# Sums of weight blocks formed from tiles already loaded, whole-tile weight loads, joins moved to the low-rank bank, four added transfers moved, one sum in four on GpSimd

## The reference, cut to what matters

```
# x: 8 batches x 512 x 2048, fp32.  R = 16
x = x + (x @ B0[i].T) @ A0[i].T                    # adapter i, one per batch
x = x + x @ W + (x @ lora_A[k]) @ lora_B[k]        # W: 2048 x 2048, adapter k per batch
```

## Time and profile before

| | |
|---|---|
| median of 3 runs | 1443.02 us (1441.91 to 1444.8) |
| profiled execution, its own time | 1451.56 us |
| its span, first to last instruction | 1449.9 us |
| TensorE busy | 1329.0 us, 92% of the span, 5684 matmuls |
| VectorE, ScalarE, GpSimd busy | 954.1, 459.2, 205.2 us |
| mean granted TensorE clock | 0.961 of full speed |
| DMA traffic | 350.93 MB, mean 242 GB/s |

### The profile page before, as it was taken

How to read it: one execution, slowest core, us unless ns; L and a number is a source line. 1 busy time by engine, 2 the same in 40 slices (tenths; PEclk the granted TensorE clock), 3 DMA queues, 4 the chain that set the end, 5 groups by cost and what they waited for, 6 DMA issues and landing times.

```text
span 1449.9 us, 15615 instructions
## 1 busy us (share of the span) xinstructions
PE 1329.0 (92%) x5684; PEld 1084.3 (75%) x5684; DVE 954.1 (66%) x1041; ACT 459.2 (32%) x536; POOL 205.2 (14%) x360
## 2 busy tenths in 40 slices
PE   6999999989788899996979999999989779999796
PEld 4888888877566688875768888888868558888585
DVE  4355755357666676765565766887877477788685
ACT  3232223222122332230322343334334235433342
POOL 3101000120123110102211100010112210100022
PEclk9999999999989999998989999999999989999899
DMA  8865843399999877888896373597898998945367
GB/s 306 283 224 168 284 145 95 110 275 361 332 373 337 276 272 255 268 280 317 275 321 218 117 246 116 181 357 249 324 348 227 249 282 213 229 150 175 94 178 170
DMA packets 140575, 350.93 MB, mean 242 GB/s; under 512 B 17476, under 2 KB 67652, under 8 KB 139476
## 3 DMA queue, kind: packets, MB, share of 16 engines
q1 hardware_dynamic: 103876, 237.01, 49.2%
q0 software_dynamic: 36624, 112.94, 26.0%
HBM read 236.55 MB, written 114.36 MB: 242 GB/s over the span
## 4 chain that ended last, share of the span: by engine, by line
PE 61%; DMA 20%; DVE 10%; issue 3%; SPq 2%; ACT 2%; POOL 1%; DVEq 0%; POOLq 0%; ACTq 0%
PE ps L2397 29%; PE ps L1247 25%; DMA w_raw<-in_W 4%; DMA wq<-in_W 3%; DMA w_ops<-job 2%; DMA w_sum<-w_raw 2%; PE ps L1220 2%; PE ps L2355 2%; DMA stage_all<-c_kept 2%; DMA job<-in_W 2%; DMA w_raw<-w_sum 1%; DVE w_lo L892 1%; ACT w_hi L733 1%; DMA lr_raw_q<-lrw 1%; PE ps L1178 1%
## 5 line engine op out<-in xcount | busy, mean ns | idle before, releaser
L1247 PE MATMUL ps<-b_hi,w_hi 128*128 128x512 f32 x896 | 359.1, 401 | 55.7 <-DVE w_lo L892 51.8
L1247 PE MATMUL ps<-b_lo,w_hi 128*128 128x512 f32 x896 | 355.6, 397 | 0.0
L1247 PE MATMUL ps<-b_hi,w_lo 128*128 128x512 f32 x896 | 354.9, 396 | 0.0
L2397 PE MATMUL ps<-b_hi,w_hi 128*128 128x512 f32 x784 | 311.3, 397 | 20.7 <-DVE val L2263 6.8
L2397 PE MATMUL ps<-b_lo,w_hi 128*128 128x512 f32 x784 | 310.0, 395 | 0.0
L2397 PE MATMUL ps<-b_hi,w_lo 128*128 128x512 f32 x784 | 309.7, 395 | 0.0
L1247 PEld LDWEIGHTS ps<-b_hi,w_hi 128*128 128x128 f32 x896 | 172.7, 193 | 100.6 <-DVE w_lo L892 58.8
L733 ACT CAST w_hi<-w_raw 128x1024 fp32r<-128x1024 f32 x88 | 92.5, 1051 | 422.1 <-PE ps L1247 203.2
L892 DVE TENSOR_TENSOR w_lo<-w_raw,w_hi 128x1024 fp32r<-128x1024 f32 x88 | 107.7, 1224 | 166.4 <-ACT w_hi L733 166.3
L1247 PEld LDWEIGHTS ps<-b_hi,w_lo 128*128 128x128 f32 x896 | 172.4, 192 | 37.1
L1247 PEld LDWEIGHTS ps<-b_lo,w_hi 128*128 128x128 f32 x896 | 172.6, 193 | 35.9
(11 more groups left out here) (151 smaller groups left out, 1186.0 us busy)
## 6 DMA issues: line engine op xcount, KB each, us to landing
w_raw<-in_W SPq DMA_DIRECT2D x88, 512.0 KB, 7.6
w_raw<-w_sum SPq DMA_DIRECT2D x56, 512.0 KB, 5.6
wq<-w_ops SPq DMA_DIRECT2D x56, 512.0 KB, 5.6
xq<-in_xT SPq DMA_DIRECT2D x44, 512.0 KB, 5.7
w_ops<-job POOLq DMA_DIRECT2D x40, 512.0 KB, 5.9
out_y<-stage POOLq DMA_DIRECT2D x40, 512.0 KB, 6.5
x_raw<-in_xT SPq DMA_DIRECT2D x32, 512.0 KB, 7.1
job<-in_W SPq DMA_DIRECT2D x24, 512.0 KB, 8.3
```

The lines of the kernel that those rows point to most:

```text
L1247: last = pe.matmul(bank[:, :], w[n % 2][:, c, t * P:(t + 1) * P], x[:, 2 * j + c, :], start=(j == 0 and c == 0 and w is w_hi and x is b_hi ...
L2397: last = pe.matmul(out, w[:, h, c, col:col + P], b[x], start=(po in (Q1, Q2, Q5, Q3) and c == 0 and i == 0), stop=(c == 3 and i == 2), ski ...
```

## The change

The jobs no longer load anything. The weight tiles of the second pair's units (56 to 111) are exactly the quarter blocks, so each stays in a place until its sums are made in it: 4 `w_raw` buffers, 3 tiles `w_more`, and for stretches of time 4 tiles in `u3`, in `x_raw[X12]` and in `x_raw[X11]`. A loop run when the program is built gives each unit a place, planning that it is free 3 units before its own. `load_weights(n + 3)` stands at the end of SyncE's iteration n and waits until the sum that was in the place is stored and read. VectorE makes js3, js1 and js2 (42 instructions) in iterations 4 to 7 of each product, GpSimd makes js4 (14 instructions) in front of its store. The additions of the identity in the jobs go, since the tiles have it already. In `two_level` a weight is one DMA of 1 MB with one semaphore, in runs of 8 KB, and the halves of a split are taken as columns of it (`w_half`). Joins write bank 1 (`p_ps`), the bank of the separate low-rank tiles, and the fourth comes one unit earlier. Four of the eight added transfers move from M6 to M3.

```diff
+    JOB_TILE = {js3: 0, js1: 4, js2: 6, js4: 2}
+    JOB_WHEN = {(js3, 0): 4, (js3, 1): 5, (js1, 0): 5, (js2, 0): 6, (js1, 1): 6, (js2, 1): 7, (js4, 0): 8, (js4, 1): 8}
+    LAST_READ = {js3: js2, js1: js1, js2: js4, js4: js4}
...
+    job_sums = {}
+    for o in range(PRODUCTS):
+        for (k, e), late in JOB_WHEN.items():
+            job_sums.setdefault(min(unit(1, o, late), LAST - 1), []).append((o, k, e))
...
+    PLACES = RAWS + 3 + 4
+    IN_U3, IN_X12, IN_X11 = "u3", "x12", "x11"
+    place_of, region_of, place_uses = {}, {}, [[] for _ in range(PLACES)]
+    free = [unit(1, P1, 0) - 2] * RAWS + [unit(0, P4, 7)] * 3 + [0] * 4
+    for n in range(unit(1, P1, 0), LAST):
+        o, u = at(n)[1:]
+        k, e = next((k, u - first) for k, first in JOB_TILE.items() if u - first in (0, 1))
+        gone = max(min(unit(1, o, JOB_WHEN[k, e]), LAST - 1) + 2.5, min(unit(1, o, JOB_WHEN[LAST_READ[k], e]), LAST - 1) + 1)
+        best = None
+        for i in range(PLACES):
+            t = i - RAWS - 3
+            regions = [(0, LAST + 9, None)] if t < 0 else [
+                (unit(1, P1, 0) + (-2 if t < 2 else 2), unit(1, P7, 3 if t < 2 else 7), IN_U3),
+                (unit(1, P7, 1 if t < 2 else 2), unit(1, P5, 1), IN_X12), (unit(1, P5, 0) - 2 + t, LAST + 9, IN_X11)]
+            for begins, ends, region in regions:
+                key = region is None, free[i], i, region
+                if free[i] <= n - 3 >= begins and gone <= ends and (best is None or key[:3] < best[:3]):
+                    best = key
+        _, _, i, region = best
+        place_of[n], region_of[n] = i, region
+        place_uses[i].append(n)
+        free[i] = gone
...
+    def w_came(n):
+        if n in place_of:
+            i = place_of[n]
+            before = len(raw_plan[i::RAWS]) if i < RAWS else 0
+            return w_loaded[i], 16 * (before + place_uses[i].index(n) + 1)
+        return w_loaded[main_raw(n)], 16 * (raw_of[n] // RAWS + 1)
...
+    def place_free(n):
+        _, o, u = at(n)
+        k, e = next((k, u - first) for k, first in JOB_TILE.items() if u - first in (0, 1))
+        return [sum_stored(n), (job_subtracted if LAST_READ[k] == js4 else job_summed, job_no[o, LAST_READ[k], e])]
+    def region_free(i, region=None):
+        return place_free([n for n in place_uses[i] if region_of[n] == region][-1])
...
-        def store_job(i, k):
-            o, h, _, _ = jobs[i]
-            tile, s, t = job_use(i, JOB_SUM[k])
-            pool.wait_ge(job_summed, job_no[i, k])
-            pool.dma_start(w_ops[o, k, :, h, :, :], tile).then_inc(job_stored[s][t], 16)
+        def store_job(o, k, e):
+            n = unit(1, o, JOB_TILE[k] + e)
+            if k == js4:
+                pool.wait_ge(job_summed, job_no[o, js2, e])
+                pool.wait_ge(w_ready, n + 1)
+                b, d = w_tile(n)[:, :, :], w_tile(unit(1, o, JOB_TILE[js2] + e))[:, :, :]
+                pool.tensor_tensor(b, b, d, ALU.subtract).then_inc(job_subtracted, 1)
+                pool.wait_ge(job_subtracted, job_no[o, k, e])
+            else:
+                pool.wait_ge(job_summed, job_no[o, k, e])
+            pool.dma_start(w_ops[FIRST_OF[o], k, :, 2 * e:2 * e + 2, :], w_tile(n)[:, :, :]
+                           ).then_inc(job_stored[place_of[n]], 16)
...
-        def load_job(i, t):
-            o, h, _, _ = jobs[i]
-            tile, s, _ = job_use(i, t)
-            for pair in job_tile_free(i, t):
-                sp.wait_ge(*pair)
-            row, col = JOB_AT[t]
-            if o in W_SUM:
-                block = w_sum[W_SUM[o]]
-                for u in (4 * row + 2 * col, 4 * row + 2 * col + 1):
-                    sp.wait_ge(*sum_kept(W_SUM[o], u))
-            else:
-                block = W[W_BLOCK[o]]
-            sp.dma_start(tile, half_of(block, row, col, h)).then_inc(job_loaded[s], 16)
+        def load_weights(n):
+            _, o, u = at(n)
+            i, region = place_of[n], region_of[n]
+            uses = place_uses[i]
+            before = uses[uses.index(n) - 1] if uses.index(n) else None
+            if before is not None and region_of[before] == region:
+                for pair in place_free(before):
+                    sp.wait_ge(*pair)
+            elif i < RAWS:
+                raw_free(max(r for r in range(len(raw_plan)) if r % RAWS == i))
+            elif region is None:
+                sp.wait_ge(*unit_end(unit(0, P4, 7)))
+                sp.wait_ge(p_added, 6)
+            else:
+                t = i - RAWS - 3
+                sp.wait_ge(*{IN_U3: (u3_stored[t // 2], 64), IN_X12: (x_ready, 4 * (PRODUCTS + P7) + t + 1),
+                             IN_X11: (x_ready, 4 * (PRODUCTS + P5) + t + 1)}[region])
+            kind = {P6: S2, P7: S3, P3: F3, P5: F5}.get(o)
+            if kind is None:
+                src = unit_of(W[{P1: A11, P2: A12, P4: A22}[o]], u)
+            else:
+                sp.wait_ge(*sum_kept(kind, u))
+                src = unit_of(w_sum[kind], u)
+            sp.dma_start(w_tile(n)[:, :, :], src).then_inc(w_loaded[i], 16)
...
-            for i, t in job_loads.get(n, []):
-                load_job(i, t)
+            if n + 3 in place_of:
+                load_weights(n + 3)
...
+                    for pair in region_free(RAWS + 3 + m // 2, IN_U3):
+                        dve.wait_ge(*pair)
...
-        def job_sum(i, k):
-            o, h, s, _ = jobs[i]
-            a, c, d, b = (job_use(i, t)[0] for t in (ta, tc, td, tb))
+        def job_sum(o, k, e):
+            n = unit(1, o, e)
+            a, c, d = (w_tile(n + u)[:, :, :] for u in (0, 4, 6))
             if k == js3:
-                dve.wait_ge(*job_loaded_for(i, ta))
-                dve.wait_ge(*job_loaded_for(i, tc))
-                if o in (M1, M4):
-                    job_eye(a, h)
+                dve.wait_ge(w_ready, n + 4 + 1)
                 dve.tensor_tensor(a, c, a, ALU.subtract).then_inc(job_summed, 1)
             elif k == js1:
-                dve.wait_ge(job_summed, job_no[i, js3])
-                dve.wait_ge(*job_loaded_for(i, td))
-                if o in (M1, M4):
-                    job_eye(d, h)
+                dve.wait_ge(w_ready, n + 6 + 1)
+                dve.wait_ge(job_summed, job_no[o, js3, e])
                 dve.tensor_tensor(c, c, d, ALU.add).then_inc(job_summed, 1)
             elif k == js2:
-                dve.wait_ge(job_summed, job_no[i, js1])
+                dve.wait_ge(job_summed, job_no[o, js1, e])
                 dve.tensor_tensor(d, d, a, ALU.add).then_inc(job_summed, 1)
...
-    fix_plan = [(4 + i // 4, i % 4 * 2, unit(M6, u)) for i, u in enumerate((4, 5, 6, 8, 9, 10, 12, 13))]
+    fix_plan = [(4 + i // 4, i % 4 * 2, unit(*at)) for i, at in enumerate(
+        ((M6, 4), (M6, 6), (M6, 8), (M6, 10), (M3, 2), (M3, 4), (M3, 7), (M3, 9)))]
...
-    join_at = {unit(M6, 0): 0, unit(M6, 2): 1, unit(M3, 13): 2, unit(M5, 2): 3}
-    j_split_at = {unit(M7, 12): 0, unit(M6, 1): 1, unit(M3, 11): 2, unit(M5, 1): 3}
+    join_at = {unit(M6, 0): 0, unit(M6, 2): 1, unit(M3, 13): 2, unit(M5, 1): 3}
+    j_split_at = {unit(M7, 12): 0, unit(M6, 1): 1, unit(M3, 11): 2, unit(M5, 0): 3}
...
-        if n in join_at:
-            r_plan.append(("join", join_at[n]))
+            r_plan += [(n // 2, 2 * (n % 2)), (n // 2, 2 * (n % 2) + 1)]
...
+    def w_half(q, h):
+        return wq[q % WEIGHTS][:, :, h * N // 2:(h + 1) * N // 2]
...
+        joins = [i for i, n in join_unit.items() if n < lr_tiles[s][0]]
+        return [(val_ready, JOINS + max(joins) + 1)] + ([] if before is None else [lr_read(before)])
...
-                for h in range(2):
-                    sp.dma_start(tile[:, h, :, :], half_of(block, i, j, h)).then_inc(w_loaded[q % WEIGHTS][h], 16)
-            else:
-                k = {Q7: 0, Q5: 1, Q6: 2, Q3: 3}[po]
-                for h in range(2):
-                    sp.wait_ge(*first.job_kept(mo, k, h))
-                    sp.dma_start(tile[:, h, :, :], w_ops[mo, k, :, h, :, :]).then_inc(w_loaded[q % WEIGHTS][h], 16)
+                src = (w_sum[W_SUM[mo]] if mo in W_SUM else W[W_BLOCK[mo]])[2 * i + j]
+            else:
+                for e in range(2):
+                    sp.wait_ge(*first.job_kept(first.product_of[mo], first.JOB[po], e))
+                src = w_ops[mo, first.JOB[po]]
+            sp.dma_start(wq[q % WEIGHTS][:, :, :], src).then_inc(w_loaded[q % WEIGHTS], 16)
...
         def join(i):
-            r = r_at["join", i]
-            for pair in r_ready(r):
-                pe.wait_ge(*pair)
+            if i % 2:
+                pe.wait_ge(val_ready, JOINS + i)
+            else:
+                before = [s for s in lr_bank if lr_tiles[s][0] < join_unit[i] and lr_bank[s] == 0]
+                pe.wait_ge(*(lr_read(before[-1]) if before else first.bank_free(first.tile(1, P5, 7))))
             pe.wait_ge(lrv_ready, JOINS + i // 2 + 1)
             pe.wait_ge(j_ready, JOINS + i + 1)
-            out = r_ps[r % 2]
+            out = p_ps
```

(34 more changed lines are left out.)

132 lines of the change are left out of this document (47 added, 85 removed).

## The result

The changed kernel took 1391.26 us (median of 4 runs, 1389.91 to 1393.82), the kernel before beside it 1443.91 us; the ratio is 0.962 (95% interval 0.956 to 0.968). That is 53 us less. In a second comparison of more rounds it was 1389.87 against 1450.37 us, ratio 0.959 (0.957 to 0.961), 60.5 us less. The prediction was 1358 us with a gain of 85 us. So the direction and the range to 1396 us hold, and the gain was 0.6 to 0.7 of what was forecast. The forecast's own range, 1340 to 1378 us, doesn't hold: 1391 us lies in the part of the range that was there for the rivals.

The account below looks back on a forecast made before the run. The prediction took the kernel as TensorE-bound except where late transfers are passed on by in-order engines; its terms, -17 - 9 - 29 - 8 - 16 - 9 + 3 = -85 us from 1443, gave 1358 us, range 1332 to 1396.

Parts of the forecast that it names:

- GpSimd holds VectorE: Rival, chance 0.08: each of GpSimd's 14 subtractions stops VectorE, costing 32 us; gain only 53 us, 1390 us.
- C: P1, second pair: fix loads no longer queue behind job loads waiting for stores; -9 of 14.0 us lost.
- E: M6 units 2 and 3: joins leave the two banks, so evictions may start earlier; -8 of 10.6 us lost.
- G: M5 units 2 and 3: joins leave the banks, the fourth a unit earlier; -9 of 13.4 us lost.
- B: End of P3 and P5, first pair: job transfers leave the full DMA; -17 of 24.7 us lost.
- D: P4 and P3, second pair: VectorE's sums no longer wait for job loads; -29 of 33.6 us lost.
- F: End of M6, begin of M4: four moved added transfers (10.8 us) and larger runs (5 us); -16 of 24.6 us lost.
- the +3 for all new waits: Allowance of 3 us for all new small waits, the last sums beside M1 included; bounds 0 and 10.
- The rule of turns: End of M6, begin of M4: 8 KB runs get a fair share beside added transfers, nearly no loss, -22 us.
- Transfers stay the bound: Rival, chance 0.15: sum stores, added transfers and loads keep B, C, E and F at cautious bounds; -47, 1396 us.
- All stalls go: Rival, chance 0.10: every stall the change can reach goes; -112 us, 1331 us.
- the places make it slower: Rival, chance 0.03: store and load in turn make each product's weights late, 15 us each; 1460 us.

Follow-up runs that it names:

- experiment 1: Changed kernel with the fourth sum of each job (14 instructions) made by VectorE, not GpSimd: 1380.78 us, ratio 0.953 to the kernel before.
- experiment 4: Changed kernel with each 1 MB second-level weight loaded as two 512 KB halves in runs of 1 KB: 1390.05 us, ratio 0.959 to the kernel before.
- experiment 2: Changed kernel with low-rank loads for M6, M4, M3 and M5.0 to M5.5 issued up to six units ahead, not two: 1373.48 us, ratio 0.948.
- experiment 7: Changed kernel with all eight fixes back in M6: 1396.84 us, ratio 0.964; kernel before with only four fixes moved to M3: 1442.57 us, ratio 0.995.
- experiment 6: Changed kernel with the sixteen uq transfers to the output in M6 and M4 written plainly, not added (output incomplete): 1367.94 us, ratio 0.943.

## Why the prediction was right, and why by less than forecast

The gain of the profiled spans fell short by 85 - 61.7 = 23 us. The steps on what the jobs and joins cost were right, and they carry most of the gain; two terms that were put at nothing or next to nothing were wrong. That 1391 us is nearly the 1390 of the rival *GpSimd holds VectorE* is chance: its mechanism is there, with 10.5 us and not 32, and other losses fill up the sum. By the prediction's steps:

- **The base.** "I take the difference to stay": 8.5 us above the median of three runs. The kernel before has since had medians of 1449 to 1452 us and a second profile of 1456.3, so it was those three runs that were low, not the profiled execution that was slow. Some 8 us of the 33 between 1358 and 1391 come from there.
- **C, E, G, the job transfers, the joins.** Right: -32 us against -26. No sum waits for a load, and the new sources of the sums cost no wait of their own. That the joins did it was read from the profiles, and so was the worth of the jobs' loads; neither was tried by itself.
- **B**, -12.9 for -17. The stall is still first-level weights from `in_W`, and the DMA share is still 0.90. In the second profile of the changed kernel B loses 7.6 us, the 8 that the prediction left. What makes the 4 us between the two profiles is open.
- **D and M1: "I take 0" for GpSimd's subtractions.** This is the first step that failed. Neither 0 nor 32 us, but 10.5 us (experiment 1). The rival had the mechanism, and its price counted every subtraction as if VectorE were always at its limit. TensorE waited only for those at P4.0 and P4.1 and at M1.1 and M1.2, where VectorE's list was full already. That these are the ends of a product, where splits, evictions, sums and the identity come together, was read in the prediction (up to 3 us late); that the subtractions fall in the same units wasn't set beside it. (Against the rival it said that VectorE is busy for 87.0 of D's 133.9 us. That is the column of the weight loads, PEld; VectorE's is 81.28. The argument is the same with it, and a mean of a stretch says nothing of its fullest units.) The rule in the Trainium skill, "SBUF — State Buffer", section "Who interferes with whom", is that a VectorE instruction with two SBUF inputs and a GpSimd instruction that reads SBUF exclude each other by a shared port pair, and that the one issued first keeps it. The trace agrees that they exclude each other: each of the stretched instructions ends about its own time after the other engine's has ended, and in 766.21 to 769.7 GpSimd's grew as well, to 3.51, behind VectorE's of 762.60. Which one keeps the ports doesn't follow from the starts in the trace: VectorE's instruction of 762.60 starts 0.3 us before GpSimd's, and is the one that waits.
- **F**, -7.5 for -16, and **the +3 for all new waits**, which came to +12.6: the main error. The forecast counted the queues' time as one sum and asked what of it comes free: 10.8 us from four moved transfers and 5 from larger runs. The runs' term had its size (5.5 us in F, experiment 4). What failed is the assumption that it takes nothing from anyone. Larger packets for SyncE's queue meant a longer wait in GpSimd's, and a 256 KB load there holds two engines' lists. It cost 9.2 us at M6.4 to M6.12 and a third of F's remaining 17.1. Issued earlier, the same loads give 17.8 us back, 15 of them here (experiment 2). The moved transfers' term was worth some 5 to 7 us (experiment 7).
- **The rule of turns.** The prediction set beside its sum the rule of the Trainium skill, "DMA: Bandwidth & Descriptors", section on queues, rings and completion order, that a DMA engine takes turns between its queues packet by packet, and gave -22 for F by it. The landings agree with the turns: M4's second weight and the added transfers take 36.2 and 10.7 us with halves, 19.0 and 30.3 with whole weights. The -22 doesn't follow, since a share that one queue gains by turns another loses. In the prediction this was read for the weights only.
- **The rivals.** "Transfers stay the bound" named F rightly and B in part; E was at its other bound. "All stalls go" and "the places make it slower" had nothing behind them: no wait of TensorE goes back to a sum's store. The nearest is the one ahead of P4.1, where a store lands at 607.4 us, and VectorE is busy until 608.0 anyway.
- **The signs.** Of those named for being wrong, two came: VectorE's 1.22 us stretched beside a subtraction, and new waits of TensorE where a product ends. Of those for being right, "those of M4 landing under 15 us" holds for the first weight (9.4 us) and not for the second (19.0).

Left open: the spread of B, and the 2.6 us of the rest. Part of the latter is M5.8 to M5.11, which differ by 4.4 us between the two profiles of the same kernel before. The wait at M6.7 was traced to the load's landing. How much of its 18.8 us the other added transfers, the stored fixes and the size of the weights' packets each make was shown for the packets (experiment 4) and the added transfers (experiment 6), not for the fixes.

## What to carry to other kernels

When one queue's transfers are made larger, ask first who is in the other queue and which engine's list stands behind its smallest load: a late load of 256 KB cost 9 us at M6.7, and to issue it some units earlier cost nothing here. An instruction given to GpSimd isn't hidden because GpSimd is idle; set its units beside VectorE's, and where VectorE is already late, let VectorE do it itself: here that was 10.5 us less. A kernel's own spread (here 1442 to 1458 us) has to be known before a profiled execution is called slow or fast.

## What the runs showed that was not expected

- A 128x1024 FP32 subtraction takes 2.36 to 3.51 us on GpSimd and 1.22 us on VectorE, and moving 14 of them to the engine with more work made the kernel 10.5 us faster.
- Loading weights in runs of 1 KB in place of 8 KB (1.8 in place of 4.7 KB a packet on average) took the landing of the other queue's added transfers from 30.3 to 10.7 us, with no change in the kernel's time; with one early load beside it the same edit cost 17 us.
- Sixteen transfers of 512 KB, in a stretch whose queues are full, cost 23 us more when they add to what lies in memory than when they write it.
